# A two-layer decoder on one core: latent attention with each pair's first scores one pair ahead, and a one-column silu in the delta stage

## The chip, the cores and the metric

The kernel runs on 1 core of one Trainium2 chip. The metric is device time in microseconds. The core's engines are TensorE (PE, with its weight loads as PEld), VectorE (DVE), ScalarE (ACT), GpSimd (POOL) and SyncE (SP), which here only issues DMAs. Each engine runs its own list of instructions in order and waits on semaphores that other engines raise. Everything is float32.

## The reference

Six sub-layers, each followed by a residual add and a layer norm, on x of 4 x 256 tokens x 256 channels. Two of them are touched: the gated delta rule (12 heads) and the latent cross attention (16 heads, keys and values made from a context of 64 channels).

```python
def _L1_attn_ref(...):                      # gated delta rule
    q = short_conv(hidden_states @ Wq, conv_wq)   # four taps, then silu
    k = short_conv(hidden_states @ Wk, conv_wk)
    v = short_conv(hidden_states @ Wv, conv_wv)
    q = l2norm(q.reshape(B, T, H, -1))
    k = l2norm(k.reshape(B, T, H, -1))
    g = -jnp.exp(A_log) * jax.nn.softplus(hidden_states @ Wa + dt_bias)
    o = gated_delta_rule(q, k, v, g, beta)

def _L1_xattn_ref(...):                     # latent cross attention
    q_hk = (hidden_q @ Wq.T).reshape(Bv, Sv, H, K)
    q_big = jnp.einsum('bshk,hkq->bshq', q_hk, w_kc_q)
    q_big = _apply_rope(q_big, sin_q[None, :, None, :], cos_q[None, :, None, :])
    kv_r = _apply_rope(kv_c, sin_k[None], cos_k[None])
    q_r = jnp.einsum('bshq,hqr->bhsr', q_big, W_qr)
    k_r = jnp.einsum('bld,hdr->bhlr', kv_r, W_kr)
    scores = jnp.einsum('bhsr,bhlr->bhsl', q_r, k_r)
    attn = jax.nn.softmax(scores, axis=-1)
    ctx_c = jnp.einsum('bhsl,bld->bhsd', attn, kv_r)
    ctx_lat = jnp.einsum('bhsd,hkd->bhsk', ctx_c, w_kc_kv)
    return ctx_lat.transpose(0, 2, 1, 3).reshape(Bv, Sv, H * K) @ Wo.T
```

## The kernel before

The six sub-layers follow each other in five functions. Each function writes the instruction lists of its engines by hand, as Python loops over small helpers; a helper waits on semaphores, issues a few instructions and raises a semaphore. So the order in which helpers are called in an engine's block is the order in which the engine works, and a helper whose semaphore is not there yet holds all that stand behind it.

**Latent attention** (first part of `latent_and_mixture`, with the mixture of 16 attention experts behind it). The heads go in 8 pairs; pair `i` has its loads, products and outputs. The matrices are absorbed first: `absorb(i)` (L2406 to L2410) multiplies the pair's query weights together, ScalarE copies them out (`copy_absorbed`, L2751 to L2755), and `output_weights(i)` (L2424) does the same for the output, copied by VectorE (`copy_mo`, L2888). Then, for two halves `c` of 512 tokens:
- `queries(i, c, n)`, n = 0 to 2 (L2433): the big queries in three parts, into banks 0, 1 and 2. VectorE multiplies each by cosines and sines (`rope`, L2896 to L2901), which frees the bank, and GpSimd adds the products (L3204).
- `latent_queries(i, c)` (L2445): six matmuls that reduce them to 64 channels per head, in bank 7, copied by ScalarE (`copy_qc`, L2761).

With these, the attention of pair `j = i - 1` runs in four blocks `b`, one per batch entry: `scores(j, b)` (L2461, banks 3 and 4), VectorE's `maximum` (L2906), ScalarE's `exp` with row sums (L2771, four calls), VectorE's `norm` (a reciprocal L2911 and four products L2917), `turn(j, b, 0)` and `turn(j, b, 1)` (L2475, four transposes each, both into bank 5), ScalarE's `copy_eT` after each (L2779), and `attend(j, b)` (L2485, bank 6). After two blocks VectorE copies the context (`copy_cx`, L2924), `outputs(j, b)` (L2502) multiplies it into bank 7, and VectorE adds that to x (`add`, L2928). Since there is one bank for transposes, the second turn waits for the copy of the first; since there is one pair of score banks, `scores(j, b)` waits for the exp of the block before. In the loop pair `i`'s queries stand between the blocks of pair `i - 1`, so all four blocks of a pair run while the queries of the next are made. After the last queries the drain works off the last pair's blocks, with a second pair of score banks and a second transpose bank; x is then normalised, transposed (L2595) and given to the experts.

SyncE loads the six weight tiles of pair `i + 1` once `absorb(i)` and `output_weights(i)` are done.

**Delta stage** (`delta_attention`). A loop over 12 heads, software-pipelined: in round `i` head `a = i + 1` is projected and convolved (`project` on TensorE L1410, `tap0` on ScalarE L1696, three taps on VectorE L1956, `silu` on ScalarE L1704), head `b = i` is transposed (L1429) and its products made, and older heads are solved. A head has four units n = 0 to 3. ScalarE also does the exponentials of the decays (`exp`, L1708), which GpSimd masks (L2185) after it made their input (`mask_g`, L2175, read by TensorE's L1417). At the end of round `i` stand `exp(a, 0)`, `exp(a, 1)` and `tap0(a, 3)`; the silu of that unit 3 follows in round `i + 1`, where `a` has become `b`, after `copy_k0`, two `square`s (L1718) and the next head's `tap0(a, 0)`. Exp and silu need different tables of ScalarE, so a table load stands before the first exp and before the first silu of each round; TensorE's L1429 for the head's second operand waits for that silu.

## Time and profile before

| | |
|---|---|
| median of the runs shown | 1564.4 us (1560.39, 1564.4, 1571.42) |
| the profiled execution | 1560.39 us, its span 1558.6 us |
| PE busy | 1295.6 us (83%), 9098 matmuls |
| DVE busy | 833.0 us (53%) |
| ACT busy | 540.4 us (35%) |
| POOL busy | 515.3 us (33%) |
| mean granted TensorE clock | 0.899 |
| delta stage | from about 485 to 930 us |
| latent attention | first query product at 941.97 us, last output product at 1309.78 us |
| costliest group | L2638, the experts' products, 153.1 us |

Times in a row are microseconds from the start of the span. A row of a time line names the engine, the line of the kernel, the operation, the tiles written and read, and how many instructions were merged; brackets give how long the engine had been idle before it and what released it. `la_area` stands for several tiles of the latent stage that share memory, `la_banks` for the eight banks of PSUM. The granted clock is a share of full speed and takes only two values in the records, 1.0 and 0.5.

### The profile page before, as it was taken

How to read it: one execution, taken by the hardware profiler on the slowest of the kernel's cores; microseconds unless marked ns; L12 is line 12 of the kernel's file. 1: busy time of each engine (PE TensorE's matmuls, PEld its weight loads, DVE VectorE, ACT ScalarE, POOL GpSimd, SP SyncE). 2: the span in 40 equal slices, each digit the busy share in tenths (PEclk: the TensorE clock that was granted, in tenths of full speed). 3: DMA queues.
4: the chain of work that ended last, by engine and by line, in shares of the span. 5: the costliest groups of instructions: out<-in, count | busy, mean ns of one | idle time of the engine just before them, and what ended most of it. 6: DMA issues, size and time to landing. Idle time of an engine off the chain costs nothing. (4 is left out here: it accounts for less than half of the span.)

```text
span 1558.6 us, 24915 instructions
## 1 busy us (share of the span) xinstructions
PE 1295.6 (83%) x9098; PEld 843.0 (54%) x9098; DVE 833.0 (53%) x1815; ACT 540.4 (35%) x1236; POOL 515.3 (33%) x596
## 2 busy tenths in 40 slices
PE   7999998343936788999999938888888877999998
PEld 4876966222523446667677824444444434444477
DVE  5365363562376667676653263565656546363433
ACT  4474562210223766566652211333232333100000
POOL 4363452406342675575571012111111111140000
PEclk9999998656876899999996767999999999999999
DMA  4000002924862011222112011000002000654100
GB/s 134 19 20 13 20 13 88 294 74 98 221 220 69 15 26 35 35 36 32 30 24 32 2 31 42 21 9 25 24 24 85 0 1 6 190 165 125 51 4 24
DMA packets 169048, 92.68 MB, mean 59 GB/s; under 512 B 91441, under 2 KB 161945, under 8 KB 168817
## 3 DMA queue, kind: packets, MB, share of 16 engines
q1 hardware_dynamic: 160784, 74.42, 18.5%
q0 software_dynamic: 4496, 13.33, 3.0%
q10 hardware_dynamic: 3664, 3.55, 0.7%
q8 instruction: 66, 1.08, 0.3%
q14 instruction: 38, 0.30, 0.1%
HBM read 76.82 MB, written 15.79 MB: 59 GB/s over the span
## 5 line engine op out<-in xcount | busy, mean ns | idle before, releaser
L2638 PE MATMUL la_banks<-la_xe,la_f_w 128*128 128x512 f32 x348 | 153.1, 598 | 3.5 <-DVE la_xe L3040 3.5
L3204 POOL TENSOR_TENSOR la_area<-la_area 128x512 f32<-128x512 f32 x48 | 60.5, 1274 | 262.7 <-DVE la_area L2897 200.0
L1956 DVE SCALAR_TENSOR_TENSOR dh_front<-dh_pj,df_conv,dh_front 128x510 f32<-128x510 f32 x144 | 107.4, 746 | 71.7 <-ACT dh_front L1696 68.1
L2638 PEld LDWEIGHTS la_banks<-la_xe,la_f_w 128*128 128x128 f32 x348 | 66.0, 192 | 84.7 <-issue 84.6
L2771 ACT ACTIVATE la_area<-la_banks,la_nmax 128x256 f32<-128x256 f32 x128 | 59.0, 473 | 145.7 <-DVE la_nmax L2906 145.7
L2433 PE MATMUL la_banks<-xT,la_area 128*128 128x512 f32 x192 | 93.8, 616 | 0.6 <-ACT la_area L2755 0.6
L337 POOL TENSOR_TENSOR wa_qkT<-wa_t_cos,wa_t_sin 128x512 f32<-128x512 f32 x40 | 50.8, 1271 | 98.7 <-DVE wa_t_sin L312 98.7
L3040 DVE TENSOR_TENSOR la_xe<-xT,la_area 128x1024 f32<-128x1024 f32 x29 | 52.5, 1828 | 56.5 <-PE la_banks L2638 49.8
L2475 PE MATMUL la_banks<-const,la_area 128*128 128x128 f32 x256 | 41.9, 291 | 46.6 <-DVE la_area L2917 31.1
L341 POOL TENSOR_TENSOR wa_masked<-wa_probs,const 128x384 f32<-128x384 f32 x64 | 63.7, 1000 | 29.9 <-ACT wa_probs L358 29.9
L2475 PEld LDWEIGHTS la_banks<-const,la_area 128*128 128x128 f32 x256 | 29.3, 146 | 77.1 <-DVE la_area L2917 41.8
L3224 POOL TENSOR_TENSOR la_o_rstd<-la_o_var,la_minus_half 128x1 f32<-128x1 f32 x8 | 6.4, 805 | 166.0 <-DVE la_o_var L3102 166.0
L2445 PE MATMUL la_banks<-la_area 128*128 128x512 f32 x96 | 57.5, 747 | 3.6 <-POOL la_area L3204 3.5
L267 PE MATMUL wa_po<-wa_wo,wa_encT 128*128 128x256 f32 x256 | 56.6, 379 | 0.0
L2691 PE MATMUL la_banks<-la_y,la_area 128*128 128x256 f32 x256 | 56.2, 379 | 0.0
L1410 PE MATMUL dh_pj<-xT,df_w 128*128 128x512 f32 x96 | 52.0, 669 | 2.8 <-PEq L133 2.8
L2917 DVE TENSOR_SCALAR la_area<-la_area,la_rec 128x256 f32<-128x256 f32 x128 | 53.4, 478 | 1.1
L2433 PEld LDWEIGHTS la_banks<-xT,la_area 128*128 128x128 f32 x192 | 34.4, 194 | 35.9 <-issue 33.9
L2691 PEld LDWEIGHTS la_banks<-la_y,la_area 128*128 128x128 f32 x256 | 48.4, 190 | 6.9 <-issue 0.5
L267 PEld LDWEIGHTS wa_po<-wa_wo,wa_encT 128*128 128x128 f32 x256 | 48.0, 190 | 6.2
L312 DVE TENSOR_TENSOR wa_t_sin<-wa_swap,const 128x512 f32<-128x512 f32 x40 | 48.4, 1210 | 0.0
L1410 PE MATMUL dh_pj<-xT,dh_w 128*128 128x512 f32 x96 | 48.2, 627 | 0.0
(565 smaller groups left out, 3039.0 us busy)
## 6 DMA issues: line engine op xcount, KB each, us to landing
placed<-mw_rows SPq DMA_DIRECT2D x8, 768.0 KB, 8.2
mw_gu<-in_L_ffn_w_gate SPq DMA_DIRECT2D x16, 384.0 KB
mw_gu<-in_L_ffn_w_up SPq DMA_DIRECT2D x16, 384.0 KB
mw_d<-in_L_ffn_w_down SPq DMA_DIRECT2D x16, 384.0 KB, 8.6
mw_rows<-placed SPq DMA_DIRECT2D x8, 768.0 KB, 5.3
la_area<-w_table POOLq DMA_DIRECT2D x6, 1024.0 KB, 12.8
la_f_w<-in_L_ffn_q_proj SPq DMA_DIRECT2D x32, 128.0 KB, 2.2
la_f_w<-in_L_ffn_k_proj SPq DMA_DIRECT2D x32, 128.0 KB, 2.4
```

The source lines that it names most:

```text
L267: mm = pe.matmul(po[:, (t + 1) % 2, 0:DIM], encT[:, i, P * t:P * t + P], wos[:, i, :], start=(i == 0), stop=(i == A_G - 1))
L341: pool.tensor_tensor(masked[:, u % 3, :], probs[:, u % 2, :], env.c("a_mask"), ALU.mult).then_inc(mask_done, 1)
L1410: mm = pe.matmul(pj[:, n % 2, :], w[a % 2][:, m, k, :], env.xT[:, k, 512 * s:512 * s + 512], start=(k == 0), stop=(k == KC - 1))
L1956: dve.scalar_tensor_tensor(dst, src[:, :, 0:SEQ - j], conv[:, a, m, D_CONV - 1 - j:D_CONV - j], dst, ALU.mult, ALU.add).then_inc(tapped, 1)
L2433: mm = pe.matmul(qb[:, n, :], wabs[:, k, n, :], env.xT[:, k, 512 * c:512 * c + 512], start=(k == 0), stop=(k == KC - 1))
L2445: mm = pe.matmul(po, mabs[:, n, :], qrot[:, c, n, :], start=(n == 0), stop=(n == 2))
L2475: mm = pe.transpose(tr[turn_bank(j, a)][:, P * (2 * l + n):P * (2 * l + n) + P], en[:, u % 2, a, n, P * l:P * l + P], env.c("ident"))
L2638: mm = pe.matmul(acc[c][m], f_w[n % SLOTS][:, m, k, :], xe[(n - U) % RING][:, k, :], start=first and k == 0, stop=last and k == KC - 1)
L2691: mm = pe.matmul(o_acc[t % 4], ae[t % RING][:, x, :], f_wo[:, x, :], start=(x == 0), stop=(x == F_E - 1))
L2771: ins = act.activation(e[:, u % 2, a, n, :], sc[bank(j, b)][:, a, n, :], ACT.Exp, bias=nmax[:, a, t:t + 1], accum_out=total[:, a, t:t + 1])
L2917: ins = dve.tensor_scalar(en[:, u % 2, a, n, :], e[:, u % 2, a, n, :], rec[:, a, 2 * b + n:2 * b + n + 1], None, ALU.mult)
L3204: pool.tensor_tensor(qrot[:, c, n, :], prod[:, c, 2 * n, :], prod[:, c, 2 * n + 1, :], ALU.add).then_inc(rotated, 1)
```

## The change

No matmul and no copy is added or taken away in the latent stage; the calls are put in another order on three engines.
- `scores(i, 0)`, `maximum(i, 0)` and `exp(i, 0)` now stand in pair `i` itself, behind the second latent product, and no longer at the start of pair `i + 1`. So each pair begins with a block whose exponentials are done.
- On ScalarE the copies of a block's transposes stand in front of the next block's exp instead of behind it, and `copy_absorbed` in front of `exp(i, 0)`.
- On TensorE four query products follow each other, and an outputs, scores or attend group stands between a block's two turns; `absorb(i + 1)` stands before the second latent product.
- The drain is written anew for this order. The memset of `lpad`, a tile of the experts' routing, moves from the drain to the start of the stage.

In the delta stage a silu of one column, whose result nobody reads, is called between `exp(a, 1)` and `tap0(a, 3)`.

```diff
@@ delta_attention @@
+        early = sb("early", [P, 1])
...
                     if a is not None:
                         exp(a, 0)
                         exp(a, 1)
+                        act.activation(early[:], env.c("ident")[:, 0:1], ACT.Silu)
                         tap0(a, 3)
@@ latent_and_mixture, TensorE @@
                 for i in range(PAIRS):
                     j = i - 1
+                    queries(i, 0, 0)
                     if j >= 0:
-                        scores(j, 0)
-                    queries(i, 0, 0)
+                        scores(j, 1)
+                        turn(j, 0, 0)
                     if j >= 1:
                         outputs(j - 1, 2)
+                    if j >= 0:
+                        turn(j, 0, 1)
                     queries(i, 0, 1)
+                    queries(i, 0, 2)
+                    queries(i, 1, 0)
+                    queries(i, 1, 1)
+                    if j >= 0:
+                        turn(j, 1, 0)
+                        scores(j, 2)
                     if j >= 1:
                         outputs(j - 1, 3)
                     if j >= 0:
-                        scores(j, 1)
-                    queries(i, 0, 2)
-                    if j >= 0:
-                        turn(j, 0, 0)
-                    queries(i, 1, 0)
-                    if j >= 0:
-                        turn(j, 0, 1)
-                        scores(j, 2)
-                    queries(i, 1, 1)
-                    if j >= 0:
+                        turn(j, 1, 1)
                         attend(j, 0)
-                        turn(j, 1, 0)
+                    queries(i, 1, 2)
                     latent_queries(i, 0)
                     if j >= 0:
-                        turn(j, 1, 1)
-                    queries(i, 1, 2)
+                        turn(j, 2, 0)
+                        scores(j, 3)
+                        attend(j, 1)
+                    if i < LAST:
+                        absorb(i + 1)
                     if j >= 0:
-                        attend(j, 1)
-                        scores(j, 3)
-                        turn(j, 2, 0)
+                        turn(j, 2, 1)
                     latent_queries(i, 1)
                     if j >= 0:
-                        turn(j, 2, 1)
+                        turn(j, 3, 0)
+                    scores(i, 0)
+                    if j >= 0:
                         outputs(j, 0)
+                        turn(j, 3, 1)
                         attend(j, 2)
                         outputs(j, 1)
-                    if i + 1 < PAIRS:
-                        absorb(i + 1)
-                    if j >= 0:
-                        turn(j, 3, 0)
-                    if i + 1 < PAIRS:
+                        attend(j, 3)
+                    if i < LAST:
                         output_weights(i + 1)
-                    if j >= 0:
-                        turn(j, 3, 1)
-                        attend(j, 3)
@@ ScalarE @@
                     if j >= 0:
-                        exp(j, 0)
-                        exp(j, 1)
                         copy_eT(j, 0, 0)
                         copy_eT(j, 0, 1)
+                        exp(j, 1)
+                        copy_eT(j, 1, 0)
+                        copy_eT(j, 1, 1)
                         exp(j, 2)
-                        copy_eT(j, 1, 0)
                     copy_qc(i, 0)
...
+                    if i < LAST:
+                        copy_absorbed(i + 1)
+                    exp(i, 0)
@@ VectorE, the drain @@
-                chain(dve.memset(lpad[:], NEG))
-                maximum(LAST, 0)
-                add(LAST - 1, 2)
                 maximum(LAST, 1)
-                add(LAST - 1, 3)
                 norm(LAST, 0)
                 maximum(LAST, 2)
                 norm(LAST, 1)
+                add(LAST - 1, 2)
                 maximum(LAST, 3)
+                norm(LAST, 2)
+                add(LAST - 1, 3)
                 copy_cx(LAST, 0)
-                norm(LAST, 2)
+                norm(LAST, 3)
                 add(LAST, 0)
                 x_stats(0)
                 x_stats(1)
-                norm(LAST, 3)
                 add(LAST, 1)
```

TensorE at the start of a middle pair, before: L2461 are scores, L2433 query products, L2502 outputs, L2475 a turn.

```order
L2461 MATMUL la_banks<-la_area 128x256 x4
L2433 MATMUL la_banks<-xT,la_area 128x512 x2
L2502 MATMUL la_banks<-la_area 128x256 x2
L2433 MATMUL la_banks<-xT,la_area 128x512 x2
L2502 MATMUL la_banks<-la_area 128x256 x2
L2461 MATMUL la_banks<-la_area 128x256 x4
L2433 MATMUL la_banks<-xT,la_area 128x512 x2
L2475 MATMUL la_banks<-const,la_area 128x128 x4
L2433 MATMUL la_banks<-xT,la_area 128x512 x2
L2475 MATMUL la_banks<-const,la_area 128x128 x4
```

And of the change (the same helpers stand two lines further down: L2463 scores, L2435 query products, L2504 outputs, L2477 turns, L2487 attend).

```order
L2435 MATMUL la_banks<-xT,la_area 128x512 x2
L2463 MATMUL la_banks<-la_area 128x256 x4
L2477 MATMUL la_banks<-const,la_area 128x128 x4
L2504 MATMUL la_banks<-la_area 128x256 x2
L2477 MATMUL la_banks<-const,la_area 128x128 x4
L2435 MATMUL la_banks<-xT,la_area 128x512 x8
L2477 MATMUL la_banks<-const,la_area 128x128 x4
L2463 MATMUL la_banks<-la_area 128x256 x4
L2504 MATMUL la_banks<-la_area 128x256 x2
L2477 MATMUL la_banks<-const,la_area 128x128 x4
L2487 MATMUL la_banks<-la_area 64x256 x4
```

The block's first turn moved from behind three query products to behind one, its second turn stands one outputs group later, and four query products are now in one row.

ScalarE in one middle pair, before, from the copies of the absorbed weights on: L2771 is exp (four calls a block), L2779 a copy of a turn, L2761 a copy of latent queries.

```order
L2755 COPY la_area<-la_banks 128x64
L2779 COPY la_area<-la_banks 128x512 x2
L2771 ACTIVATE la_area,la_total<-la_banks,la_nmax 128x256 x8
L2779 COPY la_area<-la_banks 128x512 x2
L2771 ACTIVATE la_area,la_total<-la_banks,la_nmax 128x256 x4
L2779 COPY la_area<-la_banks 128x512
L2761 COPY la_area<-la_banks 128x512
```

And of the change, two lines up (L2769 exp, L2777 copy of a turn, L2759 copy of latent queries).

```order
L2753 COPY la_area<-la_banks 128x64
L2769 ACTIVATE la_area,la_total<-la_banks,la_nmax 128x256 x4
L2777 COPY la_area<-la_banks 128x512 x2
L2769 ACTIVATE la_area,la_total<-la_banks,la_nmax 128x256 x4
L2777 COPY la_area<-la_banks 128x512 x2
L2769 ACTIVATE la_area,la_total<-la_banks,la_nmax 128x256 x4
L2759 COPY la_area<-la_banks 128x512
```

The two exps in one row are now parted by the copies of block 0's turns, and block 0's exp comes from the pair before.

ScalarE at the end of a delta round, before.

```order
L1708 ACTIVATE dh_E<-dh_tp 128x512 x2
L1696 ACTIVATE dh_front<-dh_pj,df_conv 128x512
L1713 COPY dh_k_0<-dh_tp 128x512
L1718 ACTIVATE dh_front<-dh_tp 128x512 x2
L1696 ACTIVATE dh_front<-dh_pj,df_conv 128x512
L1704 ACT_TABLE_LOAD
L1704 ACTIVATE dh_back<-dh_front 128x256
```

And of the change, where the helpers stand one line further down and L1851 is the new call.

```order
L1709 ACTIVATE dh_E<-dh_tp 128x512 x2
L1851 ACT_TABLE_LOAD
L1851 ACTIVATE dh_early<-const 128x1
L1697 ACTIVATE dh_front<-dh_pj,df_conv 128x512
L1714 COPY dh_k_0<-dh_tp 128x512
L1719 ACTIVATE dh_front<-dh_tp 128x512 x2
L1697 ACTIVATE dh_front<-dh_pj,df_conv 128x512
L1705 ACTIVATE dh_back<-dh_front 128x256
```

The table load went up by five instructions, from in front of the silu to in front of `tap0(a, 3)`; the number of table loads is the same. GpSimd's and SyncE's lists are the same as before.

## Rows read from the trace of the kernel before

**Rows 1.** Stretches: length, then busy us per engine, PEclk, DMA share.

```profile
600.00:800.00 200.00, 190.58 (x2849) 137.60 (x2848) 134.45 (x309) 124.33 (x264) 123.67 (x209) 0.97 0.21 32
...
970.60:1235.80 265.20, 225.51 (x1015) 122.65 (x1013) 152.00 (x268) 87.08 (x276) 45.42 (x36) 0.95 0.11 30
...
1235.80:1310.70 74.90, 55.66 (x262) 31.56 (x261) 43.05 (x92) 25.31 (x82) 9.68 (x8) 0.93 0.00 1
```

**Rows 2.** Waits of TensorE, 970 to 1236: total us, times, longest us.

```profile
PE la_banks L2475 <- DVE la_area L2917: 20.2, 12, 2.4
...
PE la_banks L2475 <- ACT la_area L2779: 13.5, 12, 1.3
...
PE la_banks L2485 <- ACT la_area L2779: 4.0, 6, 0.7
...
PE la_banks L2502 <- ACT la_area L2761: 2.0, 6, 0.3
```

**Rows 3.** Time line of TensorE in one latent pair: start us, us.

```profile
1057.93 1.98 PE L2433 MATMUL la_banks<-xT,la_area 128*128 128x512 f32 x4
...
1075.88 2.74 PE L2445 MATMUL la_banks<-la_area 128*128 128x512 f32 x6
...
1085.25 0.66 PE L2475 MATMUL la_banks<-const,la_area 128*128 128x128 f32 x4 [2.39 <-DVE la_area L2917]
...
1085.74 4.44 PE L2445 MATMUL la_banks<-la_area 128*128 128x512 f32 x6
```

**Rows 4.** Time lines of VectorE, GpSimd and ScalarE in the same pair.

```profile
1058.05 1.23 DVE L2906 TENSOR_REDUCE la_nmax<-la_banks 128x4 f32<-128x1024 f32 x1 [0.37 <-PE la_banks L2461]
...
1064.54 2.58 DVE L2917 TENSOR_SCALAR la_area<-la_area,la_rec 128x256 f32<-128x256 f32 x4
...
1071.69 1.14 DVE L2917 TENSOR_SCALAR la_area<-la_area,la_rec 128x256 f32<-128x256 f32 x4
...
1063.90 2.54 POOL L3204 TENSOR_TENSOR la_area<-la_area 128x512 f32<-128x512 f32 x2 [23.74 <-DVE la_area L2897]
...
1059.31 0.47 ACT L2771 ACTIVATE la_area<-la_banks,la_nmax 128x256 f32<-128x256 f32 x1 [3.51 <-DVE la_nmax L2906]
...
1060.68 0.48 ACT L2771 ACTIVATE la_area<-la_banks,la_nmax 128x256 f32<-128x256 f32 x1
...
1096.56 0.80 ACT L2751 COPY la_area<-la_banks 128x768 f32<-128x768 f32 x1 [5.27 <-PE la_banks L2410]
```

**Rows 5.** The first latent pair: its stretch, and TensorE's time line.

```profile
942.00:970.60 28.60, 24.97 (x66) 11.76 (x66) 10.04 (x17) 2.60 (x6) 7.52 (x6) 0.81 0.11 33
...
961.07 5.49 PE L2445 MATMUL la_banks<-la_area 128*128 128x512 f32 x6 [3.53 <-POOL la_area L3204]
```

**Rows 6.** Time line of ScalarE in a delta round.

```profile
714.65 0.60 ACT L1708 ACTIVATE dh_E<-dh_tp 128x512 f32<-128x512 f32 x1 [0.26 <-PE dh_tp L1417]
...
716.37 0.69 ACT L1696 ACTIVATE dh_front<-dh_pj,df_conv 128x512 f32<-128x512 f32 x1 [1.12 <-PE dh_pj L1410]
...
719.67 1.28 ACT L1704 ACT_TABLE_LOAD   x1
...
720.96 0.42 ACT L1704 ACTIVATE dh_back<-dh_front 128x256 f32<-128x256 f32 x1
```

**Rows 7.** Time lines of TensorE, VectorE and GpSimd in that round.

```profile
721.74 0.66 PE L1429 MATMUL dh_tp<-const,dh_back 128*128 128x128 f32 x4 [1.34 <-ACT dh_silu L1704]
...
717.09 2.31 DVE L1956 SCALAR_TENSOR_TENSOR dh_front<-dh_pj,df_conv,dh_front 128x510 f32<-128x510 f32 x3 [3.62 <-ACT dh_front L1696]
...
735.50 2.04 POOL L2175 TENSOR_TENSOR dh_E<-const,dh_par 128x512 f32<-128x512 f32 x2
...
739.16 1.96 PE L1417 MATMUL dh_tp<-dh_E,const 128*128 128x512 f32 x4
```

**Rows 8.** Time line of ScalarE at the start of the delta stage.

```profile
486.62 0.21 ACT L1776 ACTIVATE dh_a_exp<-df_a_log 128x12 f32<-128x12 f32 x1
...
532.76 0.69 ACT L1696 ACTIVATE dh_front<-dh_pj,df_conv 128x512 f32<-128x512 f32 x1 [0.33 <-PE dh_pj L1410]
```

56 lines of the change are left out of this document (27 added, 29 removed).

## The prediction

> **What bounds the kernel now.** I read the mean busy share by stretch first, then who waits for whom on TensorE, then the time lines of one latent pair and one delta round, since the change touches those two stages. The six middle latent pairs take 265.2 us (44.2 each), and TensorE is idle for 39.7 of them (265.2 less 225.51 busy); from the last pair's first query product to the end of the drain it is idle for 19.2 of 74.9 us; ScalarE is busy for a third of either stretch and VectorE for under 60% [rows 1]. So TensorE is the bound, and it loses 13% and 26% to waits. Its waits in the six pairs are four kinds, 39.7 us in all, on VectorE and ScalarE alone. Most are transposes (L2475) that stand in its queue in front of ready work: they wait for VectorE's normalised weights (20.2 us) and for ScalarE's copies out of the one transpose bank (13.5 us) [rows 2]. In the pair that starts at 1057.93 the longest such wait is 2.39 us, and behind it the clock falls: the same six latent products take 4.44 us at 1085.74 and 2.74 us at 1075.88 [rows 3]. The mean granted clock of 0.95 says that a tenth of the six pairs ran at the lower of the two levels (1.2 against 2.4 GHz) [rows 1]. In the delta stage TensorE is busy for 190.6 of 200 us [rows 1], with one wait of 1.34 us per round, for the silu behind a table load [rows 6, 7].
>
> **The middle latent pairs.** No matmul is added or removed, so the sum asks for TensorE's work per pair and what waits remain. Work: six pairs are 265.2 us, less 39.7 idle, less the loss to the clock (0.95 is 10% of 265.2 at half speed, so about 13 us lost): 212.5, or 35.4 a pair. With the clock's loss read from one pair instead (4.44 - 2.74 = 1.7 [rows 3]) it is 44.2 - 6.6 - 1.7 = 35.9. I take 35.5; in a queue without waits the modelled tails in front of each wait (about 0.1 each) overlap the next group, which gives 34.9.
>
> Which waits remain I find by laying a pair of the new order end to end, each group with its length from the trace. TensorE reaches, from the pair's first query product: turn(j,0,0) at 2.9, turn(j,1,0) at 11.8, turn(j,2,0) at 20.2, absorb at 23.4, the second latent product at 26.3, turn(j,3,0) at 28.9, scores(i,0) at 29.4, the next pair at 34.8 plus waits. Against that:
> - Block 0: its scores now end at 30.5 of the pair before; maximum 1.23 to 31.8; ScalarE first does a transpose copy and copy_absorbed (four copies, the first 0.80, about 1.4 in all), so exp runs from 33.3 to 35.3 (four calls 0.45 apart, 1.93) [rows 4]; normalising (0.21 + 1.14) ends at 1.9 of this pair. TensorE comes at 2.9: 1.0 to spare. Before, it waited here.
> - Block 1: exp ends at 7.4, norm starts at 8.0. GpSimd's two rope sums start at 8.1, and norm against them took 2.58, of which GpSimd covered 1.9, against 1.14 alone, while the two sums kept their 2.54 [rows 4]. Fully covered it is about 3.3, so it ends at 11.3, 0.5 before TensorE.
> - Block 2: exp ends at 17.7, norm beside two sums ends at 20.7. TensorE waits 0.6, the one wait I find.
> - Block 3 and both latent products (GpSimd's sums end over 1 us early) have 1.2 to 2.4 to spare.
> - The waits for the transpose copy vanish, since between turn(j,b,0) and turn(j,b,1) there is now an outputs, scores or attend group (about 1 us) and ScalarE is free: the copy is ahead of the next exp, no more behind 1.9 us of it. Where the spacing is tightest the margin is 0.1.
> Pair: 34.9 + 0.6 = 35.5 us, which is 8.7 less than 44.2, and **52 us** over six. The clock: every fall in these pairs follows a wait like the 2.39 us one; with 0.6 at most I expect none. The next pair's weights are asked for at a pair's start, as before, and wanted 23 us later in place of 36; no wait for a DMA is among [rows 2].
>
> A rule of the Trainium skill bears on this (SBUF — State Buffer, section on port contention): the port pair that VectorE and GpSimd share is an exclusive lock, whoever starts first keeps it for the whole instruction and the other one blocks. Taken as a full block, norm would be held for both sums: 2.5 + 1.35 = 3.9 us in place of my 3.3, so block 1 would lose 0.1 and block 2 another 0.6 per pair, 5 us in all. The row agrees in part: norm is held, but gets through in 2.58 where 1.9 of full block would need 3.0 [rows 4].
>
> **First pair, last pair and drain.** The first pair takes 28.6 us [rows 5], of which 3.53 is the wait for GpSimd before the second latent product and 2.75 the clock on it (5.49 in place of 2.74) [rows 3, 5]. Now absorb(1), 2.5 us of work, stands in front of it: 22.3, and 0.6 at the seam, so **-5.7**. In the second pair scores(0,0) has little lead; its small waits come to 1.6 us, most of it paid back by the two outputs groups (about 1 us each) that this pair does not have yet, and one clock fall beside them (1.7) is likely: **+2**. Last pair and drain: 74.9 - 19.2 idle - 5.2 (clock 0.93) [rows 1] = 50.5 of work, 48.7 without the tails of its 18 waits. The new order leaves, laid out the same way, nine waits of 0.3 to 1.0 us, 5.3 in all: the last blocks' maximum, exp and norm still follow each other, but the add of block 3 of pair 6 no longer sits between, and lpad's memset is gone from this place (0.1). With one clock fall (1.7): 55.7, so **-19**. What follows (the turn of x and the experts) starts that much earlier, unchanged: its weights are asked for by the same releases.
> Latent sum: -52 - 5.7 + 2 - 19 = **-75 us**.
>
> **The one-column silu.** It brings the silu table load (1.28 us) from its place before silu(b,3) to just behind exp(a,1) [rows 6]. Cost: exp ends at 715.25, the load and a one-column activation (0.21, that of 12 columns [rows 8]) end at 716.75, where tap0(a,3) started at 716.37 after waiting 1.12 for TensorE: 0.38 late. Gain: VectorE's three taps then end at 719.78 in place of 719.40 [rows 7], and silu starts at once, at 719.83, not at 720.96: 1.13 early. TensorE's wait of 1.34 [rows 7] shrinks to 0.2. TensorE has no other wait in a round, so it keeps what it gains, if GpSimd allows: its mask_g (735.50, 2.04) ends at 737.54, and TensorE needs it at 739.16 [rows 7], 1.6 us later; 0.38 late against 1.13 early uses 1.5. It just fits. Eight rounds have this wait; the last has a smaller one (0.4); in the first three ScalarE has only 0.33 to spare before tap0(a,3) and then runs back to back [rows 8], so the load moves and nothing is won. 8 x 1.1 + 0.4 = 9. The clock of 0.97 in [rows 1] stands for three falls, each behind this wait; I count 3 of the 5 us they cost. **-12 us**.
>
> **Sum:** -87 against the profiled execution's 1560.4 (its span plus 1.8): 1473. That run was the fastest of the three shown, 4 us below their median, so I say **1476**.
>
> **Rivals.**
> - *New waits and the clock.* The margins of 0.1 to 1.0 us fail by small latencies, TensorE waits 2 us more per pair, and the clock keeps falling once per pair (1.7): 8 x 3.7 = 30 us less gain, about 1506. For it: five margins under 0.5. Against: waits are spread, none near 2.4. 15%.
> - *The load is longer than its bar.* If ScalarE were held longer than 1.28 us, tap0(a,3) would be late by more, VectorE and GpSimd with it: 1.7 late would use up GpSimd's 1.6, and the delta stage would gain nothing, 1488. Against: silu starts at 720.96, right at the load's end [rows 6]. 8%. The Trainium skill (ScalarE: Activation LUTs, What ACT_TABLE_LOAD costs) gives 1.28 us and a drain of 1.38 with it, 2.66 per switch; by that the placement would cost this much. The trace shows the 1.28 alone.
> - *Slower: TensorE hangs on the short lead of block 0.* turn(j,0,0) is the third group of the pair, and the chain scores, maximum, exp, norm in front of it crosses three engines with 1.0 us to spare. Each us it is late beyond that costs 8 us. To lose the 87 and another 16 it would have to be 13 us late, more than the whole chain takes (8 us). 2%.
> - *No change.* The waits only move: the stage is bound by a chain per block and not by TensorE. Then a pair stays at 44, only the delta stage and part of the drain are won, 1545 to 1560. Against: the four blocks' chains overlap and VectorE is free for 40% of the time [rows 1]. 3%.
>
> **How the numbers follow.** The forecast has 72%, with 1462 to 1490 as its own range (a fall of the clock more or less in drain and delta, 0.5 us per pair either way). The first two rivals reach to 1506; so 1462 to 1505 holds over 8 in 10. A measurement can tell about 1%, 16 us. Faster by more than that: 72 + 15 + 8 = 95%; the same 3%; slower 2%.
>
> **What would show it.** Right: pairs of 35 to 36 us between first query products; no wait over 1 us on the transposes; the clock at 1.0 through the middle pairs; the latent stage's matmuls end 74 to 76 us after less start time than before; in the delta rounds the 1.34 gone and tap0(a,3) waiting on nothing. Wrong: waits of 2 us at turn(j,2,0) or turn(j,0,0), a clock of 0.95 as before, or pairs of over 39 us.

## The result, and the profile after

| | before | after |
|---|---|---|
| median of the runs measured together | 1562.39 us (4 runs) | 1473.27 us (4 runs) |
| ratio | | 0.9424, 95% interval 0.9372 to 0.9476 |
| span of the profiled execution | 1558.6 us | 1470.2 us |
| PE busy | 1295.6 us (83%) | 1259.8 us (86%) |
| mean granted TensorE clock | 0.899 | 0.912 |
| first latent query product | 941.97 us | 931.39 us |
| first latent pair | 28.66 us | 20.35 us |
| the six pairs behind it | 265.15 us | 215.76 us |
| last pair and drain, to the turn of x | 74.93 us | 54.60 us |
| from there to the end | 247.9 us | 248.1 us |

The change takes 89 us off; 1476 was forecast. The latent stage gives 78.0 of the 88.4 us by which the spans of the two profiles differ (368.74 against 290.71), the stages ahead of it 10.6. Over the latent stage TensorE's idle time fell from 62.6 to 9.4 us and its busy time, for the same matmuls, from 306.2 to 281.3 us: 53 us are waits, and 25 us are the same work done in less busy time, most of it by the higher clock.

In the views of after the latent helpers stand at L2435 (query products), L2447 (latent products), L2463 (scores), L2477 (turns), L2487 (attend), L2504 (outputs), L2777 (copies of turns), L2769 (exp), L2902 (maximum) and L2913 (norm's products).

Mean busy shares by stretch, the stretches that answer to [rows 1] and [rows 5]: delta rounds, first pair, six pairs, last pair with drain. Columns as there: length, busy us of PE, PEld, DVE, ACT, POOL, granted clock, DMA share, GB/s.

```profile
600.00:800.00 200.00, 197.55 (x3079) 142.52 (x3075) 141.96 (x330) 134.85 (x292) 131.30 (x215) 1.00 0.21 33
931.39:951.74 20.35, 19.96 (x66) 9.98 (x67) 10.20 (x15) 2.50 (x6) 7.54 (x6) 1.00 0.16 46
951.74:1167.50 215.76, 210.72 (x1012) 119.17 (x1012) 158.60 (x269) 89.41 (x283) 45.74 (x36) 1.00 0.13 37
1167.50:1222.10 54.60, 50.58 (x263) 29.12 (x262) 43.77 (x92) 23.62 (x76) 9.62 (x8) 1.00 0.00 1
```

TensorE's idle time fell from 39.7 to 5.0 us in the six pairs and from 19.2 to 4.0 us in the last stretch, and the granted clock is 1.0 in all four stretches. The largest row of TensorE's waits in the six pairs (total us, times, longest), where [rows 2] had 39.7 us in all:

```profile
PE la_banks L2477 <- DVE la_area L2913: 3.8, 7, 0.9
```

Three more waits of 0.4 to 0.8 us, and one of 0.16 and one of 0.88 in this row, belong to the first of these pairs. What is left is one wait of 0.56 us per pair, at turn(j,2,0). TensorE's time line of one pair, to be read against [rows 3]:

```profile
1023.76 1.98 PE L2435 MATMUL la_banks<-xT,la_area 128*128 128x512 f32 x4
...
1026.74 0.66 PE L2477 MATMUL la_banks<-const,la_area 128*128 128x128 f32 x4
...
1028.63 7.03 PE L2435 MATMUL la_banks<-xT,la_area 128*128 128x512 f32 x16
...
1044.72 0.66 PE L2477 MATMUL la_banks<-const,la_area 128*128 128x128 f32 x4 [0.56 <-DVE la_area L2913]
...
1050.48 2.74 PE L2447 MATMUL la_banks<-la_area 128*128 128x512 f32 x6
...
1059.70 1.98 PE L2435 MATMUL la_banks<-xT,la_area 128*128 128x512 f32 x4
```

The pair is 35.94 us long. The second latent product takes 2.74 us, not 4.44 as in [rows 3]: it runs at the higher clock. VectorE and GpSimd in the same pair, for [rows 4]:

```profile
1024.56 1.14 DVE L2913 TENSOR_SCALAR la_area<-la_area,la_rec 128x256 f32<-128x256 f32 x4
...
1031.96 3.17 DVE L2913 TENSOR_SCALAR la_area<-la_area,la_rec 128x256 f32<-128x256 f32 x4
...
1041.80 2.87 DVE L2913 TENSOR_SCALAR la_area<-la_area,la_rec 128x256 f32<-128x256 f32 x4
...
1041.45 2.54 POOL L3201 TENSOR_TENSOR la_area<-la_area 128x512 f32<-128x512 f32 x2 [2.97 <-DVE la_area L2893]
```

Norm of block 0 is alone and takes 1.14 us; those of blocks 1 and 2 stand beside two sums of GpSimd each. The four products of block 2 end at 1044.67, TensorE's turn starts at 1044.72. Narrower windows show the instructions of block 2 one by one, the two sums and then the first two of the four products:

```profile
1041.45 1.26 POOL L3201 TENSOR_TENSOR la_area<-la_area 128x512 f32<-128x512 f32 x1 [2.97 <-DVE la_area L2893]
1042.68 1.32 POOL L3201 TENSOR_TENSOR la_area<-la_area 128x512 f32<-128x512 f32 x1
...
1041.80 1.07 DVE L2913 TENSOR_SCALAR la_area<-la_area,la_rec 128x256 f32<-128x256 f32 x1
...
1042.79 1.35 DVE L2913 TENSOR_SCALAR la_area<-la_area,la_rec 128x256 f32<-128x256 f32 x1
```

The first sum ends at 1042.72 and the first product at 1042.87; the second sum ends at 1043.99 and the second product at 1044.14, both times 0.15 us later. The other two products start behind the last sum and take 0.34 us each.

In a delta round, ScalarE, then TensorE, GpSimd and TensorE again, for [rows 6, 7]:

```profile
711.93 0.60 ACT L1709 ACTIVATE dh_E<-dh_tp 128x512 f32<-128x512 f32 x1 [0.26 <-PE dh_tp L1418]
712.55 1.28 ACT L1851 ACT_TABLE_LOAD   x1
713.84 0.20 ACT L1851 ACTIVATE dh_early<-const 128x1 f32<-128x1 f32 x1
713.95 0.67 ACT L1697 ACTIVATE dh_front<-dh_pj,df_conv 128x512 f32<-128x512 f32 x1
...
717.00 0.42 ACT L1705 ACTIVATE dh_back<-dh_front 128x256 f32<-128x256 f32 x1
...
717.77 0.66 PE L1430 MATMUL dh_tp<-const,dh_back 128*128 128x128 f32 x4
...
733.23 2.05 POOL L2177 TENSOR_TENSOR dh_E<-const,dh_par 128x512 f32<-128x512 f32 x2
...
735.20 1.96 PE L1418 MATMUL dh_tp<-dh_E,const 128*128 128x512 f32 x4
```

The load starts 0.02 us after exp(a,1) ends, and the next instruction stands right behind its 1.28 us. From the end of exp(a,1) it was 1.12 us to tap0(a,3) and 5.71 to the silu ([rows 6]: 715.25, 716.37, 720.96); it is now 1.42 and 4.47 (712.53, 713.95, 717.00). TensorE's 1.34 us are gone. GpSimd's mask_g ends at 735.28, just when TensorE takes its result.

### The profile page after: what moved, and what is told of

It is laid out like the page before. It is cut to its first block and busy times, and to the rows that moved or that the text cites. A ratio compares the mean times of both kernels' runs of the same rounds, so it can differ in the third digit from the quotient of the medians.

```text
span 1470.2 us, 24927 instructions
## 1 busy us (share of the span) xinstructions
PE 1259.8 (86%) x9098; PEld 826.6 (56%) x9098; DVE 840.6 (57%) x1815; ACT 542.7 (37%) x1248; POOL 516.0 (35%) x596
## 5 line engine op out<-in xcount | busy, mean ns | idle before, releaser
L3201 POOL TENSOR_TENSOR la_area<-la_area 128x512 f32<-128x512 f32 x48 | 60.9, 1283 | 201.8 <-DVE la_area L2893 163.1
L2435 PE MATMUL la_banks<-xT,la_area 128*128 128x512 f32 x192 | 87.6, 600 | 1.4 <-ACT la_area L2753 1.4
L2777 ACT COPY la_area<-la_banks 128x512 f32<-128x512 f32 x64 | 37.3, 587 | 101.8 <-PE la_banks L2477 101.8
L2769 ACT ACTIVATE la_area<-la_banks,la_nmax 128x256 f32<-128x256 f32 x128 | 59.1, 478 | 20.4 <-DVE la_nmax L2902 20.4
L2913 DVE TENSOR_SCALAR la_area<-la_area,la_rec 128x256 f32<-128x256 f32 x128 | 62.2, 547 | 1.1
L2435 PEld LDWEIGHTS la_banks<-xT,la_area 128*128 128x128 f32 x192 | 34.7, 190 | 42.7 <-issue 40.0
L2902 DVE TENSOR_REDUCE la_nmax<-la_banks 128x4 f32<-128x1024 f32 x32 | 39.0, 1219 | 30.1 <-PE la_banks L2463 29.8
L2477 PEld LDWEIGHTS la_banks<-const,la_area 128*128 128x128 f32 x256 | 29.0, 141 | 28.2 <-DVE la_area L2913 15.1
```

The source lines that it names most:

```text
L2435: mm = pe.matmul(qb[:, n, :], wabs[:, k, n, :], env.xT[:, k, 512 * c:512 * c + 512], start=(k == 0), stop=(k == KC - 1))
L2477: mm = pe.transpose(tr[turn_bank(j, a)][:, P * (2 * l + n):P * (2 * l + n) + P], en[:, u % 2, a, n, P * l:P * l + P], env.c("ident"))
L2769: ins = act.activation(e[:, u % 2, a, n, :], sc[bank(j, b)][:, a, n, :], ACT.Exp, bias=nmax[:, a, t:t + 1], accum_out=total[:, a, t:t + 1])
L2913: ins = dve.tensor_scalar(en[:, u % 2, a, n, :], e[:, u % 2, a, n, :], rec[:, a, 2 * b + n:2 * b + n + 1], None, ALU.mult)
L3201: pool.tensor_tensor(qrot[:, c, n, :], prod[:, c, 2 * n, :], prod[:, c, 2 * n + 1, :], ALU.add).then_inc(rotated, 1)
```

## The experiments

**Theory.** The stage's length is TensorE's work plus its waits, and each wait is the distance by which one short chain (scores, maximum, exp, norm, turn, copy) comes late at one place in TensorE's list; so each of the three reorderings can be priced by laying one pair end to end. The clock falls behind waits and comes back when they go. **Rivals**: keeping TensorE's queue busy matters but not the exact places; one of the parts (the lead of block 0, the copies) makes the whole gain; the clock has its own causes. For the silu: the load must stand in ScalarE's idle time, or anywhere off the silu's path, or its true cost is above its bar.

All kernels were compared with the kernel before on the same chip. Its median was 1550.1 us beside e1 to e4, 1548.5 beside e5 to e8 and 1564.4 beside e9 to e12, so only ratios are compared across the three groups. Lengths of stretches come from each kernel's profile; those of the kernel before are given from its profile above.

**The two halves apart: e1 and e2.** e1 is the kernel before with this one line:

```diff
                         exp(a, 0)
                         exp(a, 1)
+                        act.activation(early[:], env.c("ident")[:, 0:1], ACT.Silu)
                         tap0(a, 3)
```

> The kernel before with the one-column silu alone; nothing of the latent stage is changed. Theory (the load moves into 1.12 us in which ScalarE waited anyway before tap0(a,3), and TensorE's 1.34 us wait for the silu goes in eight rounds, with the clock falls behind it): 9 to 12 us below the kernel before, delta rounds of 25.3 us instead of 26.5 and 28.15 in turn, ratio about 0.993. Rival (the load costs ScalarE more than its 1.28 us bar, GpSimd runs late and holds TensorE): no gain, ratio 1.00. In the first three delta rounds, where ScalarE has no such idle time, the theory expects no gain and up to 1 us of loss per round.

Measured: ratio 0.9888 (0.986 to 0.9916), about 17 us, more than the 9 to 12 us that were expected. The seven rounds are 25.3 us long, the first of them 24.8. e2 is the changed kernel without that line.

> The changed kernel without the one-column silu: only the latent stage is new. Theory (the two parts are 400 us apart and add up): 75 to 78 us below the kernel before, ratio 0.951, so that this and the silu alone sum to the 89 us of the whole change; latent pairs of 36.0 us. Rival (the stages interact through the time at which weights arrive or through the clock they leave behind): the two parts alone miss the whole by more than 5 us.

Measured: ratio 0.9517 (0.9481 to 0.9552), 75 us; pairs of 35.94 us. Together e1 and e2 are 5.95% of the time, the whole change (e5, below) is 5.83%: the halves add up. Seven delta rounds of either kernel, e1 ahead of e2:

```profile
609.00:785.00 176.00, 175.03 (x2734) 127.27 (x2733) 127.81 (x299) 118.71 (x260) 120.14 (x204) 1.00 0.22 34
```

```profile
609.00:785.00 176.00, 167.91 (x2598) 121.47 (x2597) 120.91 (x278) 107.24 (x234) 110.58 (x198) 0.97 0.20 31
```

TensorE was idle for 8.1 us of this stretch in e2 and for 1.0 in e1, and the clock rose from 0.97 to 1.0. Over all 14 profiles of this study, the time from the last table load ahead of the rounds to the first latent query product is 433.1 to 436.8 us in the ten kernels with the early silu in front of tap0(a,3), and 448.4, 451.2, 450.7 and 450.7 us in the three without and in e3. Seven rounds in a row take 176.7 us in those ten (177.0 in one), and 189.5 to 189.8 us in the three without, where rounds of 26.5 and 28.2 us alternate.

**Where the load stands: e3.** The changed kernel, with the line one place later:

```diff
-                        act.activation(early[:], env.c("ident")[:, 0:1], ACT.Silu)
                         tap0(a, 3)
+                        act.activation(early[:], env.c("ident")[:, 0:1], ACT.Silu)
```

> The changed kernel with the one-column silu one instruction later, behind tap0(a,3) instead of in front of it. Theory: the gain comes only from ScalarE's idle 1.12 us in front of tap0(a,3); behind it ScalarE works without a pause up to the real silu, so the load ends the silu no earlier than before: TensorE waits 1.3 us again in eight rounds and the whole gain of 9 to 12 us is lost, ratio to the kernel before about 0.950 (0.942 for the change). Rival: what counts is only that the load is no longer directly in front of the silu, and anywhere behind the exp will do: same time as the change.

Measured: ratio 0.9514 (0.9484 to 0.9543), that of e2: the gain is lost, and the rival falls. ScalarE, then TensorE, in one round of e3:

```profile
661.02 1.28 ACT L1852 ACT_TABLE_LOAD   x1
...
663.86 0.70 ACT L1697 ACTIVATE dh_front<-dh_pj,df_conv 128x512 f32<-128x512 f32 x1
664.42 0.44 ACT L1705 ACTIVATE dh_back<-dh_front 128x256 f32<-128x256 f32 x1
...
665.22 0.90 PE L1430 MATMUL dh_tp<-const,dh_back 128*128 128x128 f32 x4 [0.88 <-ACT dh_silu L1705]
```

TensorE waits 0.88 and not 1.34 us: ScalarE is not quite without a pause between tap0(a,3) and the silu in the kernel before, it waits 0.44 us for TensorE ahead of the next head's tap0, and the load now fills that. A round without a clock fall takes 26.05 instead of 26.5 us, but three of the seven still have one (27.7 us).

**A wait put back on purpose: e4.** In front of norm(j,0)'s reciprocal:

```diff
                     dve.wait_ge(exp_done, u + 1)
+                    for _ in range(3 if b == 0 else 0):
+                        chain(dve.tensor_reduce(pause[:], env.xT[:, 0, :].rearrange("p (h t) -> p h t", h=H), AX, ALU.max))
                     dve.reciprocal(rec[:, :, 2 * b:2 * b + 2], total[:, :, 2 * b:2 * b + 2]).then_inc(rec_done, 1)
```

> The changed kernel with three reductions of 128 x 1024 by VectorE, whose results nobody reads, in front of norm of block 0 in every pair: about 3.9 us on the chain of block 0, that had 1.0 us to spare by my laying out. Theory of the waits: TensorE waits 2.7 to 3.0 us at turn(j,0,0), which costs itself, 24 to 26 us over the stage, and its clock falls behind each such wait as it did behind the 2.39 us wait of the kernel before, 1.7 us each time: together 36 to 40 us, ratio to the kernel before about 0.967, pairs of 40 us, and a granted clock of 0.95 in the middle pairs. Rival A (waits of this size are harmless for the clock in the new order): 24 to 26 us and pairs of 38.3 us, clock 1.0, ratio 0.959. Rival B (block 0 has more to spare than I worked out, or the delay falls into idle time of VectorE): under 15 us.

Measured: ratio 0.9664 (0.9629 to 0.9698), and the latent stage takes 326.74 us, 36.0 more than the change. VectorE's reductions and TensorE's turn(j,0,0), then the four query products behind that turn in the same pair and in the next one:

```profile
1023.28 3.72 DVE L2909 TENSOR_REDUCE la_pause<-xT 128x4 f32<-128x1024 f32 x3
...
1028.44 0.66 PE L2478 MATMUL la_banks<-const,la_area 128*128 128x128 f32 x4 [2.70 <-DVE la_area L2916]
...
1030.33 7.03 PE L2436 MATMUL la_banks<-xT,la_area 128*128 128x512 f32 x16
...
1069.95 7.72 PE L2436 MATMUL la_banks<-xT,la_area 128*128 128x512 f32 x16
```

3.72 us put in, 2.70 us of wait: block 0 has 1.0 us to spare, as it was laid out. Two of the six pairs are 38.7 us long, the change's 35.94 plus the wait; the other four are 40.3 to 42.0, with half the clock for a while behind the wait (7.72 in place of 7.03 us above). TensorE is idle for 32.6 us of the stage against 9.4 in the change, so the waits are 23 of the 36 us and the clock is the other 13, and rival A falls. It is the price of the rival *new waits and the clock* of the prediction, whose condition the change does not meet.

**The change beside its variants: e5 and e6.** e5 is the changed kernel itself.

> The changed kernel itself, as the measure for the three runs beside it on the same chip: ratio to the kernel before 0.942 by its first measurement (0.937 to 0.948). Its latent pairs take 35.96 us with one wait of 0.56 us each, at turn(j,2,0).

Measured: 0.9417 (0.9387 to 0.9448), pairs of 35.94 us. e6 takes away the last wait:

```diff
-                        turn(j, 2, 0)
                         scores(j, 3)
+                        turn(j, 2, 0)
                         attend(j, 1)
```

> The changed kernel with scores(j,3) in front of turn(j,2,0) on TensorE, in place of behind it, in every pair. Theory of the waits: norm of block 2, which VectorE makes beside GpSimd's two sums, ends 0.6 us after TensorE comes to the turn; a scores group of 1.06 us in front of it covers that, nothing else is late, and the pairs take 35.4 us: 3 to 4 us below the change, ratio to it 0.9975, to the kernel before about 0.940. Rival (with the turn later, its copy, exp of block 3 and the turns behind them come late, and the wait only moves to turn(j,2,1) or turn(j,3,0)): no gain, pairs of 36 us.

Measured: 0.9408 (0.9376 to 0.944), which can't be told from e5. The profile does tell them apart. Four pairs of e6 as one stretch, and its turn(j,2,0):

```profile
977.10:1118.40 141.30, 141.30 (x682) 80.34 (x680) 106.99 (x181) 58.50 (x185) 30.45 (x24) 1.00 0.09 27
...
1033.81 0.66 PE L2477 MATMUL la_banks<-const,la_area 128*128 128x128 f32 x4
```

TensorE has no wait at all for four pairs, and they take 35.33 us each; the six pairs take 212.1 in place of 215.8 us. The first pair gave 1.7 us back: its 24 query products took 12.26 us, with a piece at half clock, against 10.57 in e5. In the last pair the wait only moved: its second latent product waits 0.65 us for GpSimd's sums, and the last stretch is as long as in the change (54.6 us). 35.33 us is TensorE's work in a pair in this order, without a wait.

**One part of the reordering undone at a time: e7, e8, e9.** e7, on ScalarE only:

```diff
+                        exp(j, 1)
                         copy_eT(j, 0, 0)
                         copy_eT(j, 0, 1)
-                        exp(j, 1)
+                        exp(j, 2)
                         copy_eT(j, 1, 0)
                         copy_eT(j, 1, 1)
-                        exp(j, 2)
```

> The changed kernel with only ScalarE's list changed: exp(j,1) in front of the two copies of block 0's turns and exp(j,2) in front of those of block 1, as in the kernel before. Theory of the waits: each second turn (there is one bank for transposes) waits for a copy that stands behind 1.9 us of exp: TensorE waits 2.7 us at turn(j,0,1) and 4.0 us at turn(j,1,1), 6 us per pair, 43 us over the stage, and up to 13 us more by the clock behind these waits: 43 to 56 us above the change, ratio to the kernel before 0.970 to 0.979. That would make this order the largest single part of the 78 us of the latent stage. Rival (TensorE has other work between the turns, so the copies have time): under 15 us above the change.

Measured: 0.9826 (0.9781 to 0.987), latent stage 351.63 us, 60.9 above the change; pairs of 44.3 us, as long as in the kernel before. TensorE in one pair of e7:

```profile
1040.25 0.63 PE L2477 MATMUL la_banks<-const,la_area 128*128 128x128 f32 x4 [2.52 <-ACT la_area L2777]
...
1054.25 1.09 PE L2477 MATMUL la_banks<-const,la_area 128*128 128x128 f32 x4 [3.94 <-ACT la_area L2777]
...
1057.17 3.00 PE L2435 MATMUL la_banks<-xT,la_area 128*128 128x512 f32 x4
```

The two waits are those foreseen (2.7 and 4.0), and over the stage they add the 43 us that were expected. What was too small is the clock's part, 18 us where up to 13 were said, so that the ratio lies above the expected 0.970 to 0.979: a pair is 8.4 us longer than the change's, of which the waits (less the 0.56 that they cover) are 5.9. Behind the second one, never behind the first of 2.52 us, the clock falls in every pair (3.00 us in place of 1.98 for the query product), and costs 2.5 us, not 1.7. e8, the lead of block 0 undone on three engines (TensorE's lines; VectorE's maximum and ScalarE's exp go the same way):

```diff
+                    if j >= 0:
+                        scores(j, 0)
                     queries(i, 0, 0)
...
-                    scores(i, 0)
```

> The changed kernel with scores, maximum and exp of block 0 back at the start of the next pair, on TensorE, VectorE and ScalarE; everything else as in the change. Theory of the waits: the lead of one pair is worth 2.3 us per pair (1.6 us at scores(j,1), which then waits for the exp of block 0, and three small ones) and 3 us in the drain: 16 us above the change without the clock, up to 29 us if the clock falls behind these waits too; ratio to the kernel before 0.953 to 0.961. Rival (the lead is what makes the new order work; without it the pair is as long as before): over 50 us above the change, ratio over 0.975.

Measured: 0.9541 (0.9504 to 0.9578), latent stage 305.94 us, 15.2 above the change: pairs of 38.09 us, last stretch 57.30. Its waits of TensorE in five pairs:

```profile
PE la_banks L2463 <- ACT la_area L2771: 7.4, 5, 1.5
PE la_banks L2477 <- DVE la_area L2916: 3.6, 10, 0.6
PE la_banks L2504 <- ACT la_area L2761: 1.7, 5, 0.3
```

The waits are those worked out (1.6 at the scores, and small ones), and the granted clock stays at 1.0 through these pairs. e9, the four query products in a row parted:

```diff
                     queries(i, 1, 0)
-                    queries(i, 1, 1)
                     if j >= 0:
                         turn(j, 1, 0)
-                        scores(j, 2)
...
                         turn(j, 1, 1)
+                    queries(i, 1, 1)
+                    if j >= 0:
+                        scores(j, 2)
                         attend(j, 0)
```

> The changed kernel with its four query products in a row broken up on TensorE: turn(j,1,0), outputs(j-1,3) and turn(j,1,1) stand behind three of them, scores(j,2) behind the fourth. Theory of the waits: TensorE comes to turn(j,1,0) 1.7 us earlier, when norm of block 1 is 1.3 us from its end, and block 2 is late by 1.0 in place of 0.6: 1.7 us per pair, 12 us over the stage above the change, up to 13 more if the clock falls behind these waits; ratio to the kernel before 0.949 to 0.958. Rival (the grouping only has to keep TensorE busy; where the turns stand among the products makes no difference): same as the change, ratio 0.942.

Measured: 0.9504 (0.9458 to 0.955), latent stage 302.65 us, 11.9 above the change, pairs of 37.65 us, 1.71 longer (1.7 expected), with no clock fall in them:

```profile
PE la_banks L2477 <- DVE la_area L2914: 10.7, 10, 1.2
```

**One part alone in the kernel before: e10.** On ScalarE only:

```diff
                         exp(j, 0)
-                        exp(j, 1)
                         copy_eT(j, 0, 0)
+                        exp(j, 1)
                         copy_eT(j, 0, 1)
-                        exp(j, 2)
                         copy_eT(j, 1, 0)
+                        exp(j, 2)
...
                         copy_eT(j, 1, 1)
-                        exp(j, 3)
                         copy_eT(j, 2, 0)
+                        exp(j, 3)
```

> The kernel before with one edit on ScalarE: the first copy of block 0's turns stands in front of exp(j,1), and the first of block 2's in front of exp(j,3); TensorE's and VectorE's lists are those of before. Theory of the waits: with the old list of TensorE the turns that the copies free stand in front of other late work (normalised weights 1.1 and 2.5 us late), so 1.1 us per pair is won, 8 us over the stage, ratio to the kernel before 0.995; the clock falls stay. Rival (the order of the copies is worth by itself what taking it out of the change costs): 50 us or more, ratio under 0.97.

The edit also puts the first copy of block 1 ahead of exp(j,2), which the text of the expectation does not name. Measured: 0.9936 (0.9905 to 0.9966), 10 us. In the profile the latent stage takes 351.79 us, 17 less than before: 10.8 in the six pairs, where three are 41.4 us long and the others 43.1 and 43.9, and 3.1 each in the first pair and the last stretch. The waits give 0.86 us per pair, about 5 of the 10.8; the rest is the clock, which against the expectation did not fall in the three short pairs, though each has the wait of 2.39 us. The 3.1 of the first pair is the clock and no doing of the edit: e1, whose latent stage is that of the kernel before, has 25.56 us there too. TensorE's main waits in four of its pairs:

```profile
PE la_banks L2475 <- DVE la_area L2917: 12.9, 8, 2.4
PE la_banks L2475 <- ACT la_area L2779: 3.8, 4, 1.0
```

The copies' share fell, but the turns wait for VectorE as before. So the same idea is worth 61 us when it is taken out of the change and 10 to 17 when it is put into the kernel before (where, with the old list of TensorE, only the first copy of a block goes ahead of the exp). Each place of TensorE's list waits for what comes last there, and in the old list that was mostly the normalised weights.

**The drain: e11.** The changed kernel with the old lists of the drain on TensorE and VectorE (the first lines of TensorE's):

```diff
-                scores(LAST, 1)
                 outputs(LAST - 1, 2)
-                scores(LAST, 2)
+                outputs(LAST - 1, 3)
+                scores(LAST, 1)
                 turn(LAST, 0, 0)
                 turn(LAST, 0, 1)
-                scores(LAST, 3)
+                scores(LAST, 2)
                 attend(LAST, 0)
```

> The changed kernel with the drain's lists of TensorE and VectorE as in the kernel before (as far as the lead of block 0 leaves them: its scores, maximum and exp are done ahead); the loop over pairs is that of the change. Theory of the waits: 9 us above the change by TensorE's waits at the turns of the last pair (3.3, 1.6, 2.2 and 1.1 us), and 2 to 4 more by the clock: from the last pair's first query product to the turn of x 64 to 67 us in place of 54.6 (74.9 before), ratio to the kernel before 0.947 to 0.950. Rival (the new loop alone shortens the drain, its order does nothing): 55 to 57 us, ratio 0.942.

Measured: 0.9502 (0.9461 to 0.9542), last stretch 65.74 us. The three largest waits at its turns, where 3.3, 1.6 and 2.2 us were expected:

```profile
1216.79 1.09 PE L2477 MATMUL la_banks<-const,la_area 128*128 128x128 f32 x8 [3.19 <-DVE la_area L2913]
...
1222.38 1.09 PE L2477 MATMUL la_banks<-const,la_area 128*128 128x128 f32 x8 [0.80 <-DVE la_area L2913]
...
1227.73 1.60 PE L2477 MATMUL la_banks<-const,la_area 128*128 128x128 f32 x8 [2.17 <-DVE la_area L2913]
```

TensorE is idle for 11.7 us of the stretch, not 4.0, and the clock (0.95 over it) is most of the rest. Of the 20.3 us that the last pair and the drain lost, the new order of the drain is 11.1, and the loop's new order, with the lead, is 9.2.

**What no run takes apart.** VectorE's list of the loop is new too, which the shortened diff ahead of the prediction does not show: norm(j,0) stands in front of the pair's first rope and no longer behind the second, norm(j,1) and norm(j,2) each stand one or two ropes earlier, and add(j-1,3) later. The largest waits of before were for just these norms, and how much of the gain needs this order no run tells. The place of absorb(i+1), which is to cover the first pair's wait of 3.53 us, was not tested by itself either; in the profile of the change that wait is gone.

**What the one wait waits for: e12.**

```diff
-                            pool.tensor_tensor(qrot[:, c, n, :], prod[:, c, 2 * n, :], prod[:, c, 2 * n + 1, :], ALU.add).then_inc(rotated, 1)
+                            w = 512 if i == 0 else 32
+                            pool.tensor_tensor(qrot[:, c, n, 0:w], prod[:, c, 2 * n, 0:w], prod[:, c, 2 * n + 1, 0:w], ALU.add).then_inc(rotated, 1)
```

> The changed kernel in which GpSimd adds only 32 of the 512 columns of the rope products from the second pair on; the latent queries of these pairs are made from old sums, so this part of the computation is left out. Theory (the one wait left, 0.56 us at turn(j,2,0), comes from norm of block 2 being held by GpSimd's sums): norm takes 1.14 us in every block, the wait goes, pairs take 35.3 us, 4 us less in all, ratio to the kernel before 0.939. Rival (exp of block 2 or VectorE's own queue makes it late): the wait stays above 0.3 us, pairs of 35.8 us or more.

This kernel leaves out most of the sums, so it does not compute the layer; it serves for its time alone. Measured: 0.9378 (0.9339 to 0.9418), latent stage 285.23 us, 5.5 below the change; pairs of 35.17 us without a wait. Norm of block 2, and a pair of the short sums:

```profile
1039.63 1.14 DVE L2913 TENSOR_SCALAR la_area<-la_area,la_rec 128x256 f32<-128x256 f32 x4
...
1038.57 0.46 POOL L3202 TENSOR_TENSOR la_area<-la_area 128x32 f32<-128x32 f32 x2 [4.87 <-DVE la_area L2893]
```

So the 0.56 us are norm of block 2 being held by GpSimd, and nothing else. The pair is shorter by 0.77 us, more than the wait that the profile shows. One pair at full clock in e10 (TensorE's old list, six waits), in the change (one wait) and in e12 (none), with the same matmuls; the second number is the length, the third TensorE's busy time:

```profile
1063.20:1104.62 41.42, 35.80 (x172) 20.02 (x170) 25.34 (x45) 14.31 (x46) 7.56 (x6) 1.00 0.08 23
...
1023.76:1059.70 35.94, 35.38 (x172) 20.09 (x170) 26.75 (x46) 14.63 (x47) 7.62 (x6) 1.00 0.10 27
...
1022.03:1057.20 35.17, 35.17 (x173) 20.17 (x171) 23.11 (x46) 14.46 (x47) 1.48 (x6) 1.00 0.10 28
```

The busy time falls by 0.63 us from six waits to none, about 0.1 us for each: the modelled ends of the matmuls in front of a wait count as work in the profile and overlap the next group when the wait goes.

## Why the prediction was right, point by point

- **What bounds it.** Right: removing TensorE's waits shortened the stage by as much (53 us), and most of the other 25 us is the clock behind them. The granted clock in the middle pairs went to 1.0, as was said. A slip: 39.7 of 265.2 us are 15%, not the 13% of the text; nothing was worked out from it.
- **The middle pairs.** The one remaining wait was named with its place and size (0.6; 0.56). The work term was mis-sized: 34.9 us without tails, where e12, without a wait, takes 35.17, and 35.33 in e6's order. The deduction for tails (0.6) was right in size: a pair at full clock with the old list is busy for 35.80 us (e10), 0.63 more than in e12. What was too low is the 35.5 from which it was taken off. The mean over the six pairs includes the second pair, which lacks two outputs groups and is busy for 1.7 us less than the next (0.3 us a pair); the reading from one pair, 35.9, was the right one. A pair is 35.17 us of work and 0.77 for the one wait with the tail in front of it, 35.94 and not 35.5 us, and the six pairs gave 49.4 us where 52 less the 2 of the second pair was said.
- **The margins.** Block 0's 1.0 us is what e4 measured. Block 1 fits. The two norms beside two sums take 3.17 and 2.87 us for the four products, and norm of block 1 as a whole 3.37 (1031.76 to 1035.13) where about 3.3 was said. The single instructions under "The result" say what the norms wait for: each product that stands beside a sum ends 0.15 us after that sum, in all 343 such cases of the 13 profiles with whole sums, so VectorE gets one product through between two sums and does two behind the second, 0.68 us after it (1044.67 against 1043.99). The prediction worked with a rate instead, and its 3.3 for block 1 came out close all the same, by luck. The Trainium skill (SBUF — State Buffer, section SBUF: two separate sides) has the port pair that VectorE and GpSimd share as an exclusive lock for a whole instruction. The trace agrees with that, instruction by instruction; what did not come is the 5 us that the prediction worked out from it, because it let no product through between the two sums.
- **First pair.** -8.3 us against -5.7. The 22.3 us of work that were left after taking out one wait and 2.75 us of clock still had more of the lower clock in it (0.81 over the stretch in [rows 5]). At full clock the work is 20 us. How low the clock was there is chance: with the same list the first pair takes 25.56 us in e1 and in e10, and against these the change gains 5.2 us. So 3.1 us of this term, and of the 78.0 of the stage, are luck of the profile before.
- **Second pair.** Its small waits came (1.7 us more than a later pair's, paid back by the two outputs groups it lacks), but no clock fall: it took 36.08 us, +0.1 and not +2.
- **Last pair and drain.** -20.3 against -19. Seven waits of 0.2 to 0.9 us, 4.0 in all, where nine with 5.3 were laid out, and the clock fall of 1.7 did not come; against that the work is 50.6 us and not 48.7, so here the 1.8 us taken off for tails did not show. The two places with the longest waits in all:

```profile
PE la_banks L2477 <- DVE la_area L2913: 1.4, 3, 0.6
PE la_banks L2504 <- DVE la_area L2920: 1.0, 2, 0.8
```

- **The silu.** The mechanism holds in every number: tap0(a,3) 0.30 late (0.38 said), the silu 1.24 early (1.13), the wait gone, GpSimd just in time, and hardly anything won ahead of the seven rounds (0.5 us in the mean, where the eighth of the eight rounds lies too). The term was too small: -12 was said, and over the 14 profiles it is -15.4 us (434.7 against 450.1 in the mean). The missing piece is mostly the clock: three falls in the seven rounds, 5 us, all came back, where 3 was counted, and what lies behind the seven rounds gained 2 us instead of 0.4. The profiled pair shows only 13.4 of it, and 10.6 at the latent stage's start, since that execution entered the delta stage 2.8 us later.
- **The sum.** -75 and -12 against -78.0 and -10.6 in the two profiles. The misses are small and partly cancel: the middle pairs 2.6 us too short, two clock falls counted (3.4 us, in the second pair and in the drain) that were not there, the drain's work 1.9 us too low, and the 3.1 us of chance in the first pair. That 1476 lies 3 us from the median of 1473.3 is closer than the terms are.
- **The rivals.** *New waits and the clock*: the waits needed for it are not there, but e4 shows that its price was right, 36 us for a wait of 2.7 us at one turn per pair. *The load is longer than its bar*: it is 1.28 us and nothing follows it. The Trainium skill (ScalarE: Activation LUTs, What ACT_TABLE_LOAD costs) adds a drain of 1.38 us to each switch; no gap of that kind stands around any load shown here. *Slower* and *no change*: nothing of either.

What stays open: why the clock fell behind some waits and not behind others of the same size (below), why the first latent pair and the first delta rounds differ by some 3 us between executions of the same code, and what VectorE's new order in the loop is worth by itself.

## What to carry to other kernels

Where one engine is the bound and has idle time, lay one period of its list end to end and write beside each instruction when its inputs are there; the waits of the new order, their places and their sizes come out to a few tenths of a microsecond, and parts of a reorder must be priced together, since a part that is worth 61 us inside the new order was worth 10 to 17, in nearly the same form, in the old one. Put copies that free a single bank ahead of long work on their engine, put a table load into a gap of its engine and not merely off the critical instruction, and take one period's work from a steady period at full clock, not from a mean over unequal ones; here some 0.1 us went with each wait that went in the middle pairs. Where two engines hold each other up, look at their instructions one by one: merged rows looked like a slower pace and were one instruction let through at a time. Price the clock beside the waits, from a row at either level, and expect all of it back when the waits go.

## What was not expected of the hardware

- The size of a wait alone did not tell whether the clock fell behind it. In e3 it fell in three of seven delta rounds, each with a wait of about 0.9 us. In e8 it fell in none of the middle pairs, each with one of 1.5 and several smaller, and in e7 behind none of the waits of 2.52 us and behind each one of 3.94. In the kernel before it fell behind all seven waits of 2.4 us, in e10 behind three of seven. In e4 four of six waits of 2.7 to 2.9 us were followed by half clock. A fall cost 1.6 to 1.7 us in most places and 2.5 us per pair in e7.
- The same instructions start the latent stage at different clocks: the first pair takes 28.66 us in the kernel before and 25.56 in e1, and 20.35 to 23.11 in the kernels with the new order.
- The stretch ahead of the seven delta rounds (from the same table load, the first four rounds in it) took from 110.4 us (the kernel before) to 114.0 us (e2) with the same code; 1.5 of the 3.6 us are that one of GpSimd's masks came 2.6 or 4.1 us after TensorE was ready for it. Behind the latent stage, e3 took 243.7 us from the turn of x to the end and the change, with the same code there, 248.1. A single pair of profiles can mislead by this much on a gain of 15 us.
- Four products of VectorE, 1.14 us alone, took 2.87 and 3.17 us beside two sums of GpSimd. Each product beside a sum ended 0.15 us after it; the sums took 1.26 and 1.32 us, against 1.27 for one alone, so it is VectorE that pays.
